# Moving the weight preparation of an eight-core transformer kernel: casts and transposes ahead of the scale scans, scans in smaller pieces on the SyncE queue, loads released by the tile

## The reference

```python
x = x + attn_a(_layernorm(x), W_in, b_in, short_w, short_b, inner_w, inner_b, W_out, b_out)
x = x + ffn(_layernorm(x), W1, b1, W2, b2)
x = x + attn_b(_layernorm(x), W_qkv, b_qkv)
x = x + ffn(_layernorm(x), W1, b1, W2, b2)
```

```python
w_scale = jnp.clip(jnp.mean(jnp.abs(W)), EPS, None)
Wq = _ste(W, jnp.clip(jnp.round(W / w_scale), -1.0, 1.0) * w_scale)
```

## Time and profile before

| | us |
|---|---|
| median of 2 runs | 8230.9 |
| the two runs | 8146.63 and 8315.17 |
| the profiled execution | 8152.43 |
| its span, slowest core | 8150.9 |
| spans of the eight cores | 8126.0 to 8150.9 |
| preparation (first instruction to the first load of x) | 577.7 |
| first layernorm and its transposes | 577.7 to 656 |

### The profile page before, as it was taken

One profiled execution on the slowest core, in us unless ns is written; L12 is line 12 of the kernel. 1 busy time (PEld: TensorE's weight loads), 2 busy tenths in 40 slices (PEclk: granted clock), 3 DMA queues, 4 the chain that ended last, 5 costly groups with the idle time before them and its releaser, 6 DMA issues.

```text
span 8150.9 us, 61679 instructions; the slowest of 8 cores (8126.0 to 8150.9 us)
## 1 busy us (share of the span) xinstructions
PE 4399.7 (54%) x20936; PEld 1899.2 (23%) x21256; DVE 2068.7 (25%) x2655; ACT 2087.6 (26%) x5784; POOL 61.5 (1%) x112
## 2 busy tenths in 40 slices
PE   0217745455566744455465963455465963555466
PEld 0113312122223321222222321222222321222222
DVE  5402023333001213333102113333201123333300
ACT  1325403333004112333103522333202221333300
POOL 1010000000000000000000000000000000000000
PEclk9999877677787877777787986777787976777778
DMA  6653340000322121000223242000222112000132
GB/s 215 219 122 101 101 157 24 31 31 29 116 83 74 58 100 40 31 31 24 98 93 107 87 128 97 31 31 31 78 93 95 38 67 98 31 31 24 45 110 85
DMA packets 259912, 629.19 MB, mean 77 GB/s; under 512 B 59794, under 2 KB 125458, under 8 KB 240147
## 3 DMA queue, kind: packets, MB, share of 16 engines
q1 hardware_dynamic: 239412, 541.32, 19.6%
q0 software_dynamic: 20192, 83.90, 3.8%
HBM read 478.37 MB, written 163.58 MB: 79 GB/s over the span
## 4 chain that ended last, share of the span: by engine, by line
PE 42%; DMA 19%; DVE 17%; ACT 13%; issue 5%; SPq 2%; DVEq 0%; ACTq 0%; POOL 0%; POOLq 0%
PE psC L775 7%; DMA xring<-xscr_a 6%; PE psA L705 6%; PE psD L775 5%; DMA hiTb<-hiT_s 5%; PE psB L705 5%; DVE hib L731 3%; DVE colA L723 3%; ACT hB L728 3%; ACT hstage L741 3%; DMA wload<-W 2%; PE psA L532 2%; PE psB L532 2%; DVE kiH L730 2%; DMA xring<-x_in 2%
## 5 line engine op out<-in xcount | busy, mean ns | idle before, releaser
L705 PE MATMUL psA<-t1b,xiT 128*128 128x512 bf16 x1982 | 669.0, 496 | 549.6 <-ACT hB L712 444.8
L775 PE MATMUL psC<-t2b,hiTb 128*128 128x512 bf16 x2004 | 560.7, 445 | 625.9 <-DMA hiTb<-hiT_s 621.7
L300 PE MATMUL psT<-identt,xib 128*128 128x128 bf16 x256 | 37.4, 300 | 1311.3 <-DVE xib L691 1311.3
L705 PE MATMUL psB<-t1b,xiT 128*128 128x512 bf16 x1990 | 558.9, 426 | 3.3 <-issue 0.3
L682 DVE TENSOR_REDUCE colA<-xlnf 128x1 f32<-128x1024 f32 x64 | 78.1, 1220 | 1689.9 <-ACT xlnf L679 1689.9
L775 PE MATMUL psD<-t2b,hiTb 128*128 128x512 bf16 x2004 | 450.8, 379 | 2.3
L775 PEld LDWEIGHTS psC<-t2b,hiTb 128*128 128x128 bf16 x2048 | 222.8, 111 | 950.6 <-issue 790.1
L705 PEld LDWEIGHTS psA<-t1b,xiT 128*128 128x128 bf16 x2048 | 219.6, 117 | 888.6 <-issue 795.1
L712 ACT ACTIVATE hB<-psA,ws_pp 128x512 f32<-128x512 f32 x256 | 175.9, 687 | 842.8 <-DVE hib L731 422.6
L783 DVE SCALAR_TENSOR_TENSOR oring<-psC,ws_pp,xring 128x512 f32<-128x512 f32 x64 | 48.0, 750 | 1199.6 <-PE psC L779 1199.6
L274 ACT ACT_TABLE_LOAD x3 | 3.8, 1283 | 1282.8 <-DVE colA L273 1282.8
(11 more groups left out here) (183 smaller groups left out, 6203.1 us busy)
## 6 DMA issues: line engine op xcount, KB each, us to landing
xring<-xscr_a SPq DMA_DIRECT2D x192, 512.0 KB, 5.7
hiT_s<-hstage SPq DMA_DIRECT2D x64, 1024.0 KB, 4.8
hiTb<-hiT_s SPq DMA_DIRECT2D x64, 1024.0 KB, 6.2
winb<-win_s SPq DMA_DIRECT2D x60, 1024.0 KB, 5.9
wload<-W POOLq DMA_DIRECT2D x24, 2048.0 KB, 9.5
xring<-x_in SPq DMA_DIRECT2D x64, 512.0 KB, 4.1
xscr_a<-oring SPq DMA_DIRECT2D x64, 512.0 KB, 2.9
t1b<-t_s SPq DMA_DIRECT2D x16, 2048.0 KB, 16.5
```

Source lines behind the costliest of these rows:

```text
L300: (lambda e, b=b, j=j, ps=ps: e.matmul(ps[:, (b - j) * 128:(b - j + 1) * 128], src_fn(b), identt[:], start=True, stop=True)),
L705: P.op("tensor", (lambda e, dcc=dcc, hc2=hc2, ps=ps: e.matmul(ps[:, 0:512], xiT[:, dcc * 128:(dcc + 1) * 128], t1b[:, dcc * H + hc2 * 512: ...
L775: P.op("tensor", (lambda e, hcc=hcc, eh=eh, ps=ps, slh=slh: e.matmul(ps[:, 0:512], hiTb[:, slh * H + hcc * 128: slh * H + (hcc + 1) * 128] ...
```

## The change

Five things are changed.

- W_in and W_qkv (stages 5 and 6) are put ahead of the scale passes. The W_qkv loads go to a part of `stage` that their own transposes do not fill (`wqload2`) and do not wait for the stores of W_in.
- `wscale_pass` loads pieces of 512 KB (128 x 1024) instead of 2 MB, 64 in all, from SyncE's queue, into two slots of a buffer of its own, `wscan`.
- In `tern_build` the loads wait for `buf_guard` and the first transposes for `stage_guard`. W1: no guard for the loads, `stq` for the transposes. W2: the end of W1's transposes (`e1`) for the loads, `st1` for the transposes.
- `ln_transpose_all` in both attention sublayers takes `tile_deps`: with them the loads of x wait for the store of their own tile, and the operations of `ln_tile` are made without the gate. The transposes keep the gate.
- The driver passes `tile_deps` to all sublayers; they are empty for the very first.

```diff
+        for part in range(3):
+            for i in range(DC):
...
+                ldc = dma("gpsimd", wq_s, W_in[i * 128:(i + 1) * 128, part * D:(part + 1) * D], deps=dep)
+                stc = dma("sync", win_s[i * 128:(i + 1) * 128, part * D:(part + 1) * D], wq_s, deps=[ldc])
...
+        wqload2 = stage[:, DC * E3:DC * E3 + 2 * D]
+        q_guard = [None, None]
+        for i in range(EC3):
...
+            ld = dma("gpsimd", wq_s, W_qkv[i * 128:(i + 1) * 128, :], deps=dep)
...
+        stq = dma("sync", wqkvT_s.rearrange("(dc p) e -> p dc e", p=128), stage[:, 0:DC * E3], deps=[lastq])
...
-                ld = dma("gpsimd", w_s, src, deps=[slot_guard[par]])
+            for k, src in enumerate(chunks):
+                par = k % 2
+                w_s = wscan[:, par * 1024:par * 1024 + 1024]
+                dep = [slot_guard[par]] if slot_guard[par] else []
+                ld = dma("sync", w_s, src, deps=dep)
...
-        def tern_build(W_ap, wsi, ntiles, tilecols, nblk, col_of, guard):
+        def tern_build(W_ap, wsi, wsi_done, ntiles, tilecols, nblk, col_of, buf_guard, stage_guard):
...
-                    [t])
+                    [t] + sg)
+                sg = []
...
+        e1 = tern_build(W1, ws1i_pp, ws1_done, H // 128, D, DC, lambda i, b: b * H + i * 128, None, [stq])
+        e2 = tern_build(W2, ws2i_pp, ws2_done, D // 128, H, HC, lambda i, b: b * D + i * 128, e1, [st1])
...
-            sl, ld = load_x_tile(ring_in, xring, i, src_ap, start_deps)
+            ng = bool(tile_deps)
+            td = [tile_deps[i]] if tile_deps else list(start_deps)
+            sl, ld = load_x_tile(ring_in, xring, i, src_ap, td, nogate=ng)
```

More of the change, by code:

```diff
@@ L265, in build_nc, with ln_tile @@
     ring_o = Ring(2)
-    def ln_tile(xt_ap, out_ap, deps, par=0):
+    def ln_tile(xt_ap, out_ap, deps, par=0, nogate=False):
         o6, o2 = par * 12, par * 2
         pA, pB, pC = colA[:, par:par + 1], colB[:, par:par + 1], colC[:, par:par + 1]
[L270 to L277, removed]
+        s0 = P.op("vector", lambda e: e.bn_stats(st6[:, o6:o6 + 6], xt_ap[:, 0:512]), deps=deps, fence=True, nogate=nogate)
+        s1 = P.op("vector", lambda e: e.bn_stats(st6[:, o6 + 6:o6 + 12], xt_ap[:, 512:1024]), deps=deps + [s0], fence=True, nogate=nogate)
+        s2 = P.op("vector", lambda e: e.bn_aggr(st2[:, o2:o2 + 2], st6[:, o6:o6 + 12]), deps=[s0, s1], fence=True, nogate=nogate)
+        s3 = P.op("vector", lambda e: e.tensor_single_scalar(pA, st2[:, o2 + 1:o2 + 2], EPS_LN, OP.add), deps=[s2], fence=True, nogate=nogate)
+        s4 = P.op("scalar", lambda e: e.activation(pA, pA, AF.Ln), deps=[s3], fence=True, nogate=nogate)
+        s5 = P.op("scalar", lambda e: e.activation(pB, pA, AF.Exp, scale=-0.5), deps=[s4], fence=True, nogate=nogate)
+        s6 = P.op("vector", lambda e: e.scalar_tensor_tensor(pC, st2[:, o2:o2 + 1], -1.0, pB, OP.mult, OP.mult), deps=[s5, s2], fence=True, nogate=nogate)
+        return P.op("scalar", lambda e: e.activation(out_ap, xt_ap, AF.Identity, bias=pC, scale=pB), deps=[s6] + deps, nogate=nogate)
     def load_x_tile(ring, buf, i, src_ap, extra=(), nogate=False):
@@ L382, in build_nc @@
          nc.sbuf_tensor("stage", [128, DC * H], BF16) as stage, \
+         nc.sbuf_tensor("wscan", [128, 2 * 1024], F32) as wscan, \
          nc.sbuf_tensor("wqload", [128, 2 * D], BF16) as wqload:
+        wc_prev = [None, None]
+        wc_last = None
+        for part in range(3):
+            for i in range(DC):
+                par = i % 2
+                wq_s = wqload[:, par * D:(par + 1) * D]
+                dep = [wc_prev[par]] if wc_prev[par] else []
+                ldc = dma("gpsimd", wq_s, W_in[i * 128:(i + 1) * 128, part * D:(part + 1) * D], deps=dep)
+                stc = dma("sync", win_s[i * 128:(i + 1) * 128, part * D:(part + 1) * D], wq_s, deps=[ldc])
+                wc_prev[par] = stc
+                wc_last = stc
@@ new lines, in build_nc @@
+        lastq = None
+        wqload2 = stage[:, DC * E3:DC * E3 + 2 * D]
+        q_guard = [None, None]
+        for i in range(EC3):
+            par = i % 2
+            wq_s = wqload2[:, par * D:(par + 1) * D]
+            dep = [q_guard[par]] if q_guard[par] else []
+            ld = dma("gpsimd", wq_s, W_qkv[i * 128:(i + 1) * 128, :], deps=dep)
+            lastq = transpose_blocks(
+                lambda bb, wq_s=wq_s: wq_s[:, bb * 128:(bb + 1) * 128], DC,
+                (lambda e, bb, pc, ps, i=i: e.copy(stage[:, bb * E3 + i * 128: bb * E3 + i * 128 + 128], ps[:, pc:pc + 128])),
+                [ld])
+            q_guard[par] = lastq
@@ L385, in wscale_pass @@
+        stq = dma("sync", wqkvT_s.rearrange("(dc p) e -> p dc e", p=128), stage[:, 0:DC * E3], deps=[lastq])
         def wscale_pass(W_ap, ntiles, tilecols, ws_pp, wsi_pp, guard):
-            z = P.op("vector", lambda e: e.memset(accv[:], 0.0), deps=[guard])
+            z = P.op("vector", lambda e: e.memset(accv[:], 0.0), deps=[guard] if guard else [])
             prev = z
             slot_guard = [guard, guard]
[L389 to L394, removed]
-                ld = dma("gpsimd", w_s, src, deps=[slot_guard[par]])
+            W_v = W_ap.rearrange("(a p) d -> p a d", p=128)
+            chunks = []
+            if tilecols >= 1024:
+                for a in range(ntiles):
+                    for d0 in range(0, tilecols, 1024):
+                        chunks.append(W_v[:, a:a + 1, d0:d0 + 1024])
+            else:
+                ga = 1024 // tilecols
+                for a0 in range(0, ntiles, ga):
+                    chunks.append(W_v[:, a0:a0 + ga, :])
+            for k, src in enumerate(chunks):
[3 more added lines that the diff above has]
+                ld = dma("sync", w_s, src, deps=dep)
@@ L421, in tern_build @@
                 t_s = tern[:, par * H:par * H + tilecols]
-                ld = dma("gpsimd", w_s, W_ap[i * 128:(i + 1) * 128, :], deps=[ld_guard[par]])
-                a = P.op("vector", lambda e, tc=tilecols, w_s=w_s: e.tensor_scalar(tA[:, 0:tc], w_s, wsi[:, 0:1], 0.5, OP.mult, OP.is_gt), deps=[ld, t_prev])
-                b = P.op("vector", lambda e, tc=tilecols, w_s=w_s: e.tensor_scalar(tB[:, 0:tc], w_s, wsi[:, 0:1], -0.5, OP.mult, OP.is_lt), deps=[ld, t_prev])
+                gd = [ld_guard[par]] if ld_guard[par] else []
+                ld = dma("gpsimd", w_s, W_ap[i * 128:(i + 1) * 128, :], deps=gd)
+                a = P.op("vector", lambda e, tc=tilecols, w_s=w_s: e.tensor_scalar(tA[:, 0:tc], w_s, wsi[:, 0:1], 0.5, OP.mult, OP.is_gt), deps=[ld, t_prev, wsi_done])
+                b = P.op("vector", lambda e, tc=tilecols, w_s=w_s: e.tensor_scalar(tB[:, 0:tc], w_s, wsi[:, 0:1], -0.5, OP.mult, OP.is_lt), deps=[ld, t_prev, wsi_done])
                 ld_guard[par] = b
@@ L430, in tern_build, with ln_transpose_all @@
                     (lambda e, bb, pc, ps, i=i: e.copy(stage[:, col_of(i, bb):col_of(i, bb) + 128], ps[:, pc:pc + 128])),
-                    [t])
+                    [t] + sg)
+                sg = []
                 tern_guard[par] = last_ev
             return last_ev
-        e1 = tern_build(W1, ws1i_pp, H // 128, D, DC, lambda i, b: b * H + i * 128, ws2_done)
+        e1 = tern_build(W1, ws1i_pp, ws1_done, H // 128, D, DC, lambda i, b: b * H + i * 128, None, [stq])
         st1 = dma("sync", t1_s.rearrange("(dc p) h -> p dc h", p=128), stage[:, 0:DC * H], deps=[e1])
-        e2 = tern_build(W2, ws2i_pp, D // 128, H, HC, lambda i, b: b * D + i * 128, st1)
+        e2 = tern_build(W2, ws2i_pp, ws2_done, D // 128, H, HC, lambda i, b: b * D + i * 128, e1, [st1])
         st2_ = dma("sync", t2_s.rearrange("(hc p) d -> p hc d", p=128), stage[:, 0:HC * D], deps=[e2])
[L439 to L460, removed]
     prep_done = [st1, st2_, stq, bw1, bw2, wc_last, l_bin, l_sw, l_sb, l_iw, l_ib,
                  l_bqk, l_bo, l_bv, l_id, l_ca, ws1_done, ws2_done]
-    def ln_transpose_all(src_ap, start_deps, xlnT):
+    def ln_transpose_all(src_ap, start_deps, xlnT, tile_deps=None):
         slot_guard = [None, None]
@@ L470, in ln_transpose_all @@
             xl_s = xlnt[:, par * D:(par + 1) * D]
-            sl, ld = load_x_tile(ring_in, xring, i, src_ap, start_deps)
+            ng = bool(tile_deps)
+            td = [tile_deps[i]] if tile_deps else list(start_deps)
+            sl, ld = load_x_tile(ring_in, xring, i, src_ap, td, nogate=ng)
             ap = ln_tile(xring[:, sl * D:(sl + 1) * D], xl_s,
-                         [ld] + ([slot_guard[par]] if slot_guard[par] else []), par)
+                         [ld] + ([slot_guard[par]] if slot_guard[par] else []), par, nogate=ng)
             ring_in.use(sl, ap)
@@ L481, in ln_transpose_all, with sublayer_attn_a @@
         return trs
-    def sublayer_attn_a(src_ap, dst_ap, start_deps):
+    def sublayer_attn_a(src_ap, dst_ap, start_deps, tile_deps=None):
         stores = []
@@ L491, in sublayer_attn_a @@
              rsb("diag4", [128, DC * 4 * 128], BF16) as diag4:
```

(5 more changed lines are left out.)

5 lines of the change are left out of this document (3 added, 2 removed).

## The result

| | before | changed |
|---|---|---|
| profiled execution | 8152.4 | 8219.5 |
| span, slowest core | 8150.9 | 8217.9 |
| first load of x, median of the eight cores | 577.2 | 638.6 |
| median of all runs (10 and 11) | 8227.8 | 8303.9 |
| span of a die that kept its clock, median | 8132.6 | 8189.4 |

The account below looks back on a forecast made before the run. Waits were taken to bound the kernel: stages follow one another, and the preparation is one chain that nothing hides. Sum: 8152.4 + 12 (preparation) - 7 (three seams) = 8157 us, range 8115 to 8250.

Parts of the forecast that it names:

- The chain: Preparation: stays one chain that nothing hides, scans not beside the casts; 589.8 us instead of 577.7, 12 us longer.
- The rival of scans beside casts: Preparation: scans run beside the casts thanks to their own buffer; 155 us less, 8002, 1.8% faster; chance 0.02.
- The front: Start to first store of W_in, behind ten small loads on SyncE's queue: 22 us, bounds 15 and 43.
- the 6 us that the freed W_qkv loads should give: W_in and W_qkv: W_qkv loads go out at 465.3 instead of 471.6, 6 us less, bounds 0 and 7.
- `stq`: Store after W_qkv's last transpose: stays bare, all 19.2 us counted, since the first scan load waits behind its bytes.
- The scans: Scale passes: 64 pieces at 2.43 us, from the statistics pass, 155 us against 137 before; alternative row 3.2 each, 206.
- W2: W2's ternary tiles: 12 MB beside the store need 37 us; stage 88 us, 12 less, bounds 5 and 22.
- The seams: Three seams between sublayers: x load goes out behind the last store's issue, 2.3 us each, 7 less, bounds 0 and 10.
- The serial scan loads: Scans: loads do not overlap, 5.0 us a piece, 320 us in all; 165 more, 8322, 2.1% slower; chance 0.03.
- the hidden layernorms: Sublayer joints: layernorms run beside the end of the feed-forward sublayer; 222 less, 7935, 2.7% faster; chance 0.02.
- the slower scan with 8229: Preparation: scan at the W1 tiles' pace and small loads holding the queue to 43 us; 51 + 21 more; chance 0.12.
- The range: Whole kernel: 8115 to 8250 us; within 2% (163 us) of before with chance 0.95.

Follow-up runs that it names:

- e4: The kernel before with scan pieces of 512 KB instead of 2 MB, two slots, still from GpSimd's queue: ratio 1.0081, 3.14 us a piece.
- e7: The changed kernel with the scan loads written between the casts of W_in and W_qkv, four slots, W2's loads waiting for `st1`: ratio 0.9918 to the kernel before.
- e2: The changed kernel with 2 MB scan pieces from GpSimd's queue into `wload`, W1's loads waiting for the scans: ratio 1.0105 to the kernel before.
- e3: The changed kernel with the 512 KB scan pieces in four slots instead of two: 1.88 us a piece, ratio 1.0005 to the kernel before.
- e6: The changed kernel with only W2's first two loads allowed beside the store `st1`: W2's stage 99 us, ratio 1.0040 to the kernel before.

## Why the forecast was right or wrong

**The chain.** Right. No scan began before `stq` had landed, the preparation stayed one chain, and e4 and the table behind e7 show that its length goes into the total one for one. The rival of scans beside casts did not happen in the changed kernel, for the reason given; e7 shows what it would have been worth.

**The front.** Right: 21.4 us for 22, so the small loads were slow only beside the 2 MB loads. (In e4, with 512 KB loads beside them in their old place, SyncE's queue was through with them at 24.4 us instead of 42.8.) From there to `stq` 4 us were missed: of the 6 us that the freed W_qkv loads should give, 2 came.

**`stq`.** Right: bare, 20.1 us, and e2 shows the other side: a load on the other queue, issued before, need not wait (first reduction at 201.8).

**The scans: a term that was mis-sized.** I took 2.43 us a piece from a row of the statistics pass, whose loads land in 3.4 us. The scan's loads land in 3.8, and the pace was 2.74: 20 us, with 2 more until the first piece was there. The mechanism, the round trip of a slot, was right (e3). The step "I take 155, from the row with the same queue" chose the row of other data over the one of the same weights; the truth lay between 2.43 and 3.2, two fifths of the way.

**W2: a step that failed.** "12 MB need 37 us": that is what 12 MB take (e6: 37.4). But nothing in the changed kernel holds the third, fourth and fifth load. Each waits only for VectorE to have read the tile two before it, which it does under the store; so 18 MB shared the engines instead of 12, and the store took 61.6 us. The error was to count the loads that the change releases and not those which they release in turn. And had I counted only two, the 88 would still have been wrong, since the third tile comes late then (99 us, e6). The right forecast was a loss of 15 us or a draw, and its bound of "5 less" reached neither. Behind the store the stage went as priced, 54 us for 51.

**The seams.** The place was right, the size not: 0.6 to 0.9 us each for 2.3. The load starts sooner by the time the store takes to land, but behind the store's own 512 KB. I had written for `stq` that a transfer waits for the bytes ahead of it, and did not apply it here.

**The rivals.** The serial scan loads and the hidden layernorms did not happen. The one that came nearest is the slower scan with 8229, but its other half, a queue held to 43 us, did not happen; what stood in its place was W2. I had no rival for the store that is starved.

**The range.** That "within 2%" came true says little for the sum: it allows 163 us either way, and the two missed terms have the same sign. 8249 as the sum of the unfavourable bounds held the profiled execution (8219.5) but not the median of all runs.

## What to carry to other kernels

A pass of load and reduce in two slots is paced by the round trip: load latency plus reduction, over the number of loads in flight. Make the pieces smaller only with more of them in flight (here 2.74 us with two, 1.88 with four, for the same 512 KB). Before letting loads go out beside a store that others wait for, count every load that is then free to go, the ones behind the first included (here five for two); and a buffer of its own overlaps nothing while its load stands behind a waiting store on an in-order queue.

## What the runs showed of the hardware that was not expected

- Two DMA queues under way at once did not share the engines evenly: GpSimd's loads of W2, in 2 MB pieces, had 65 to 72% of the engines' time from 518 to 553 us and SyncE's 8 MB store 28 to 33%. In the first 19 us, with both of the first loads under way, the loads had 47% and the store 52%. Why is not shown.
- The same 512 KB piece went at 3.14 us in two slots from GpSimd's queue (e4) and at 2.74 from SyncE's. The two runs differ in place as well, so the queue alone is not shown to be the cause.
- The profile counts a load that casts f32 to bf16 by the bytes it writes: 74 GB/s for the 85.3 us of W_qkv's stage are 6.3 MB, its 24 tiles of 256 KB. It reads twice that. By the f32 bytes it is 148 GB/s at 49% of the engines' time, which is the price of the plain 512 KB scans, 190 GB/s at 62%. So the 133 and 74 GB/s of the two cast stages look slower than they are, and the casts cost the engines what their source bytes cost.
